# Levels two and four tiles behind as overlaid broadcast rows in a gated linear attention layer on one Trainium2 core

## The chip, the cores and the metric

The kernel runs on one core of one Trainium2 chip, in one launch. Its engines are TensorE (PE, with its weight loads shown as PEld), VectorE (DVE), ScalarE (ACT), GpSimd (POOL) and SyncE (SP), which here only issues DMAs. The metric is the device time of the launch in microseconds, lower is better. The kernel before takes 1411.46 us, the median of 3 runs (1408.34 to 1414.47).

## The reference

Input x is 8 sequences of 1024 tokens with 128 features. Per sequence, with 8 heads of size 128 and 12 decay levels:

```python
q, k, v = x @ Wq.T, x @ Wk.T, x @ Wv.T            # per head 128 wide; x is layernormed first
g   = -softplus(x @ Wg.T + bg);  G = cumsum(g)     # one gate per head
lam = softplus(x @ Wdl.T + Lparam)                 # one weight per head and level
lvl[t, s] = 0 if t == s else floor(log2(t - s)) + 1
A[t, s] = (q[t] . k[s]) / sqrt(128) * exp(G[t] - G[s]) * lam[t, lvl[t, s]]   for s <= t
out = layernorm((A @ v) @ Wo.T + x) * ln_g + ln_b;  x = x0 + out
# then a second layernorm, a gate over 8 experts (top 2, renormalized) and the weighted sum of their linear maps
```

What matters here is the weight W[t, s] = exp(G[t] - G[s]) * lam[t, lvl]. The kernel makes its logarithm and takes one exp. A tile of 128 keys times 128 queries that lies d tiles behind the diagonal holds levels as follows: d = 0 and 1 hold many; d = 2 holds levels 8 and 9 (distances under and from 256), d = 3 holds level 9 alone, d = 4 holds levels 9 and 10 (distances under and from 512). Tiles five and more behind hold level 10 alone and are handled by running states.

## The kernel before

The sequences are a batch loop b of 8, the heads a loop of 8 inside it, 64 heads in all, numbered n. The work of a head is cut into 12 groups (GROUPS: one key tile and up to 512 queries; nine of them are SPLIT and computed in high and low parts, three are FULL and 128 wide), and each group into 4 places, so a head has 48 places and a sequence 384. Each engine runs its own program over the same places; tables written out by hand (U_AT, FAR_AT, V_AT, PE_MORE, DVE_MORE, ACT_MORE, POOL_MORE) say at which place it does an extra piece. Engines are in order, and semaphores join them. Per group: PE makes scores (`scores`, L1523 to L1525 or L1577) into one of two banks s_ps; DVE multiplies them with the weights (`weigh`, L1150) into one of 7 buffers a; ACT rounds them (`high_a`, L892); POOL subtracts (`low_a`, L692); PE multiplies with the values (`values`, L1603 or L1598) LAG = 6 groups behind the scores.

The weights w of head n+1 are made while head n runs. `unit(n, u)` on PE (L1546) builds the logarithms by small fp16 matmuls against masks into l_ps, in four units: d = 0 (16 matmuls), d = 1 (16), d = 2 (8, 96 columns) and d = 4 (8, 64 columns). `exps(n, u)` on ACT (L844) turns each tile into w by one exp of 128x128 with the key's bias: 8, 7, 6 and 4 of them. For d = 3 no matmul is needed: `far_exps` (L855) does 5 exps from a row of logarithms that a DMA spreads over all partitions (far, 320 KB). The operands of the matmuls are small tables (ra, rc, rb) gathered by 8, 8 and 16 DMAs a head from scratch in DRAM (`load_low`, L456; `load_rb`, L469), all issued by SP in the order of `load_levels`, three heads ahead; `load_next_farther` (L483) waits for cq_done, which PE gives at place 41 (`state_values`, L1625). DVE's first `weigh` of a head waits until all exps of that head are done.

Once per sequence the pieces of the tables run: layernorm statistics (`first_statistics`, `second_statistics`, L1163), `take_y` on ACT (L941, waits for the output store of the sequence before last), the gates of the experts (`gates`, L1333 to L1359), softplus, sums, logs, decays, `low_logs` (L1249) on DVE, and 16 pieces `add_up` (`up`, L1376 and L1379).

Of the kernel before, what the change touches and what calls it, by code (L numbers as in the profile page):

```python
# [22 lines left out]
H = 8  # L23
# [27 lines left out]
F16 = mybir.dt.float16  # L51
BF16 = mybir.dt.bfloat16
# [20 lines left out]
UNITS = [[(0, 0, 8)], [(1, 1, 7)], [(2, 2, 6)], [(4, 4, 4)]]  # L73
# [13 lines left out]
def constants():  # L87
# [38 lines left out]
def program(nc, x, Wq, Wk, Wv, Wg, bg, Wdl, Lparam, Wo, ln_g, ln_b, fWg, fbg, fWe, fbe, masks, table, out):  # L126
# [4 lines left out]
    eb_dram = nc.dram_tensor("eb_scratch", [B, H * HIGH, 2, T], F16, kind="Internal").ap()  # L131
    ef_dram = nc.dram_tensor("ef_scratch", [B, HIGH * H + H, NF], F32, kind="Internal").ap()

    with ExitStack() as outer:
# [15 lines left out]
        def m(name, rows_=P):  # L150
# [3 lines left out]
                   m_dram, n_dram, ea_dram, eb_dram, ef_dram, cst, mask, m, c, rows,  # L154
# [6 lines left out]
LAG = 6  # L161
# [19 lines left out]
HALF_B = TB // 2  # L181
# [16 lines left out]

PE_MORE = {4: [('Y', 0)], 33: [('Y', 1)], 59: [('T', 0)], 87: [('Z', 0)], 93: [('T', 1)], 118: [('Z', 1)],
# [14 lines left out]
ACT_MORE = {8: [('y', 0)], 32: [('t_apply', 0)], 36: [('y', 1)], 47: [('t_apply', 1)], 54: [('t_apply', 3)],  # L214
            56: [('t_apply', 2), ('t_high', 0)], 107: [('t_high', 1)], 112: [('apply2', 0)], 122: [('x_high', 0)],
            123: [('apply2', 3), ('x_high', 1)], 132: [('abs', 0)], 145: [('num', 0)], 159: [('exp', 0)],
            171: [('ln', 0)], 198: [('lnl', 0)], 217: [('l_high', 0)], 239: [('l_high', 1)], 328: [('ek', 0)]}
POOL_MORE = {23: [('t_dev', 0)], 41: [('xb', 0), ('dev1', 0)], 43: [('apply1', 1), ('apply1', 0)],
             54: [('apply1', 2)], 55: [('apply1', 3)], 60: [('scale', 0)], 75: [('scale', 1), ('xb', 1)],
             78: [('add', 0)], 82: [('add', 1)], 93: [('dev2', 0)], 103: [('apply2', 1)], 121: [('apply2', 2)],  # L220
             268: [('total', 0)], 301: [('base', 0)], 374: [('total', 1)], 376: [('base', 1)]}
# [50 lines left out]
def main_stage(nc, x, Wq, Wk, Wv, Wg, bg, Wdl, Lparam, Wo, ln_g, ln_b, fWg, fbg, fWe, fbe, masks, table, out,  # L272
# [3 lines left out]
    with ExitStack() as ctx:  # L276
# [1619 lines left out]
```

## Time and profile before

| | before |
|---|---|
| median of 3 runs | 1411.46 us |
| profiled execution, its own time | 1405.15 us |
| span of the profiled execution | 1403.3 us |
| PE busy | 1299.5 us (93%), 10278 matmuls |
| PEld busy | 1137.4 us (81%) |
| DVE busy | 1082.8 us (77%), 2724 instructions |
| ACT busy | 1104.5 us (79%), 3270 instructions |
| POOL busy | 792.7 us (56%), 956 instructions |
| mean granted clock of PE | 0.987 |
| moved by DMA | 80.37 MB, mean 57 GB/s |

The profile is of one execution. Busy time is the union of an engine's instructions; matmuls are pipelined and their ends are modelled, so a PE that is busy all the time may still wait, and starts tell more than lengths. "Idle before" is charged to whatever released the engine. In steady state one sequence of 8 heads repeats every 165.3 us.

### The profile page before, as it was taken

The page shows a single profiled execution, that of the slowest core. Times are in us where ns is not written, and L with a number is a line of the kernel's source. Part 1 is how long each engine was busy: PE and PEld are TensorE (multiplying, and loading weights), DVE is VectorE, ACT ScalarE, POOL GpSimd, SP SyncE. Part 2 cuts the span into 40 slices and gives each one's busy share as a digit, 9 for nine tenths or more (in the row PEclk, how much of TensorE's full clock was granted, in tenths as well). Part 3 has the DMA queues.
Part 4 walks back from the last instruction along what each step waited for, and adds up shares of the span by engine and source line. Part 5 has one row for each costly group of instructions (what it writes and reads, how often), then busy time and mean ns, then how long its engine had stood idle before and what let it go on. Part 6 is the DMA issues. An engine that isn't in the chain of part 4 may idle for free.

```text
span 1403.3 us, 31442 instructions
## 1 busy us (share of the span) xinstructions
PE 1299.5 (93%) x10278; PEld 1137.4 (81%) x10278; DVE 1082.8 (77%) x2724; ACT 1104.5 (79%) x3270; POOL 792.7 (56%) x956
## 2 busy tenths in 40 slices
PE   4699899999999999999999999999999999989997
PEld 4588788888888788787888888887888878878875
DVE  4767767798868977689777988679886797767776
ACT  3589879888788877897788977888778887778732
POOL 2154457734585455953578444864558545595562
PEclk9899999999999999999999999999999999999998
DMA  5311122112221121111221122211212112211200
GB/s 180 113 45 51 43 70 70 42 43 59 58 72 44 50 73 54 44 50 44 73 73 50 44 58 58 67 44 37 71 46 73 50 44 59 72 45 30 67 9 16
DMA packets 125725, 80.37 MB, mean 57 GB/s; under 512 B 50569, under 2 KB 115323, under 8 KB 125435
## 3 DMA queue, kind: packets, MB, share of 16 engines
q1 hardware_dynamic: 124472, 77.85, 20.2%
q8 instruction: 83, 1.36, 0.4%
q10 hardware_dynamic: 1090, 0.51, 0.2%
q14 instruction: 80, 0.65, 0.2%
HBM read 67.64 MB, written 10.09 MB: 55 GB/s over the span
## 4 chain that ended last, share of the span: by engine, by line
PE 47%; ACT 16%; DVE 12%; POOL 11%; SPq 6%; issue 4%; DMA 3%; ACTq 0%; POOLq 0%; DVEq 0%
PE o_ps L1603 11%; ACT w_all L844 6%; PE s_ps L1523 4%; PE l_ps L1546 4%; PE aux L1523 4%; PE s_ps L1525 4%; PE s_ps L1524 4%; POOL a_lo_all L692 4%; PE aux L1524 3%; PE aux L1525 3%; SPq L456 3%; ACT a_hi L892 3%; DVE a_all L1150 2%; PE aux L1616 2%; SPq L469 2%
## 5 line engine op out<-in xcount | busy, mean ns | idle before, releaser
L692 POOL TENSOR_TENSOR a_lo_all<-a_all,a_hi 128x256 fp32r<-128x256 f32 (+2 forms) x576 | 575.5, 1016 | 526.2 <-ACT a_hi L892 524.4
L844 ACT ACTIVATE w_all<-l_ps,bias 128x128 f32<-128x128 f32 x1589 | 439.3, 388 | 43.8 <-PE l_ps L1546 42.4
L1150 DVE TENSOR_TENSOR a_all<-s_ps,w_all 128x512 f32<-128x512 f32 (+3 forms) x768 | 360.6, 483 | 132.6 <-PE s_ps L1525 87.9
L1603 PE MATMUL o_ps<-a_hi,v_all 128*128 128x256 f32 (+2 forms) x1152 | 396.7, 353 | 1.7 <-POOL a_lo_all L692 1.7
L892 ACT ACTIVATE a_hi<-a_all 128x256 fp32r<-128x256 f32 (+2 forms) x576 | 300.1, 547 | 75.5 <-DVE a_all L1150 73.7
L1523 PE MATMUL s_ps<-q_hi,xt_hi 128*128 128x256 f32 (+2 forms) x576 | 224.8, 390 | 31.1 <-DVE a_all L1150 29.3
L1603 PEld LDWEIGHTS o_ps<-a_hi,v_all 128*128 128x128 f32 x1152 | 218.1, 189 | 23.1 <-POOL a_lo_all L692 1.8
L1525 PE MATMUL s_ps<-q_hi,xt_lo 128*128 128x256 f32 (+2 forms) x576 | 195.1, 339 | 0.0
L1524 PE MATMUL s_ps<-q_lo,xt_hi 128*128 128x256 f32 (+2 forms) x576 | 194.7, 338 | 0.0
L1603 PE MATMUL o_ps<-a_lo_all,v_all 128*128 128x256 f32 (+2 forms) x576 | 194.4, 338 | 0.0
L1523 PEld LDWEIGHTS s_ps<-q_hi,xt_hi 128*128 128x128 f32 x576 | 109.8, 191 | 43.9 <-DVE a_all L1150 22.8
L884 ACT ACTIVATE v_all<-aux 128x512 fp32r<-128x512 f32 x124 | 79.1, 638 | 56.7 <-PE aux L1525 56.7
L1603 PEld LDWEIGHTS o_ps<-a_lo_all,v_all 128*128 128x128 f32 x576 | 109.8, 191 | 11.5
L1525 PEld LDWEIGHTS s_ps<-q_hi,xt_lo 128*128 128x128 f32 x576 | 108.9, 189 | 7.9
L1076 DVE CAST q_hi<-aux 128x512 fp32r<-128x512 f32 x128 | 88.0, 687 | 35.2 <-PE aux L1525 34.8
L1379 DVE SCALAR_TENSOR_TENSOR late<-aux,gl,late 128x128 f32<-128x128 f32 x392 | 110.8, 342 | 5.4 <-PE aux L1525 5.4
L1524 PEld LDWEIGHTS s_ps<-q_lo,xt_hi 128*128 128x128 f32 x576 | 110.1, 191 | 4.6
L855 ACT ACTIVATE w_all<-far,bias 128x128 f32<-128x128 f32 x320 | 101.0, 413 | 0.0
L1119 DVE TENSOR_TENSOR v_all<-aux,v_all 128x512 fp32r<-128x512 f32 x128 | 87.5, 684 | 7.1 <-ACT v_all L884 6.8
L1089 DVE TENSOR_TENSOR q_lo<-aux,q_hi 128x512 fp32r<-128x512 f32 x128 | 88.5, 691 | 4.4
L1523 PE MATMUL aux<-nt,xt_hi 128*128 128x256 f32 x256 | 73.1, 286 | 10.6 <-DVE tx L1249 3.8
L1577 PE MATMUL s_ps<-q_full,x_full 128*128 128x128 f32 x384 | 79.6, 289 | 1.5 <-DVE a_all L1150 1.5
(259 smaller groups left out, 2617.5 us busy)
## 6 DMA issues: line engine op xcount, KB each, us to landing
far<-ef_scratch SPq DMA_DIRECT2D x64, 320.0 KB, 3.6
rb<-eb_scratch SPq DMA_DIRECT2D x1016, 0.8 KB
farther<-ef_scratch SPq DMA_DIRECT2D x64, 192.0 KB, 3.3
ra<-ea_scratch SPq DMA_DIRECT2D x508, 4.0 KB, 2.1
rc<-ea_scratch SPq DMA_DIRECT2D x508, 4.0 KB, 1.6
mt<-m_scratch SPq DMA_DIRECT2D x62, 128.0 KB, 3.5
nt<-n_scratch SPq DMA_DIRECT2D x62, 128.0 KB, 3.5
tx<-in_L_attn_x SPq DMA_DIRECT2D x9, 512.0 KB, 5.6
```

What stands on the lines that cost most here:

```text
L692: pool.tensor_tensor(a_lo[r][:, 0:t1 - t0], a[r][:, 0:t1 - t0], a_hi[r][:, 0:t1 - t0].bitcast(F32), ALU.subtract).then_inc(a_lo_done, 1)
L844: last = act.activation(w[k][:, W_AT[j] + d, :].rearrange("p (f c) -> p f c", f=2), l_tiles[:, :, :, i - i0], ACT.Exp, bias=bias[b % 2][:, ...
L855: last = act.activation(w[k][:, W_AT[j] + FAR0, :], far[k][:, j * P:(j + 1) * P], ACT.Exp, bias=bias[b % 2][:, h, BIAS_AT[FAR0] + j:BIAS_A ...
L892: act.activation(a_hi[r][:, 0:t1 - t0], a[r][:, 0:t1 - t0], ACT.Copy).then_inc(a_hi_done, 1)
L1076: dve.tensor_copy(q_hi[n % 2][:, cols], bank(piece)).then_inc(q_hi_done, 1)
L1089: dve.tensor_tensor(q_lo[n % 2][:, cols], bank(piece), q_hi[n % 2][:, cols].bitcast(F32), ALU.subtract).then_inc(freed(piece), 1)
L1150: dve.tensor_tensor(a[(n * NG + g) % NA][:, 0:t1 - t0], s_ps[:, g % 2, 0:t1 - t0], w[n % 2][:, at:at + (t1 - t0) // P, :].rearrange("p i n ...
L1379: ins = dve.scalar_tensor_tensor(acc[:, i, :], bank(piece)[:, k * P:(k + 1) * P], gl[0][:, i, ex:ex + 1], acc[:, i, :], ALU.mult, ALU.add)
L1523: pe.matmul(o, a_hi, hi, start=True, stop=False)
L1524: pe.matmul(o, a_hi, lo, start=False, stop=False)
L1525: return pe.matmul(o, a_lo, hi, start=False, stop=True)
L1603: last = pe.matmul(o, lhs[:, vr, j, :], rhs[r][:, 0:t1 - t0], start=fresh, stop=True, skip_group_check=True)
```

## The change

Five things change together.

1. The units d = 2 and d = 4 on PE, their tables rb, masks mb2 and mb4, scratch eb, their 16 DMAs a head and their exps from PSUM go. In their place three rows of logarithms (levels 8, 9 and 10, of 6, 6 and 4 tiles: row8, row9, row10) are spread over all partitions by three DMAs a head, into one buffer each (before: two buffers of far).
2. DVE overlays: by `copy_predicated` with a fixed 128x128 mask of bytes it writes the level 9 row over row8 (6 tiles, 768 elements a partition) where the distance is in level 9, and over row10 (4 tiles, 512 elements) where it is still in level 9. It does so once each a head, at places 20 and 15.
3. ACT does 5, 6 and 4 exps from row9, row8 and row10 (`row_exps`) after groups 3, 6 and 9; before, 6 and 4 from PSUM and 5 from far. The next rows are fetched only when all three sets of exps of the head before are done.
4. LAG is 7 and there are 8 buffers each of a, a_hi and a_lo.
5. All tables of places are new. `low_logs` and `level_high` have one part instead of two.

```diff
-LAG = 6
+LAG = 7
-UNITS = [[(0, 0, 8)], [(1, 1, 7)], [(2, 2, 6)], [(4, 4, 4)]]
+UNITS = [[(0, 0, 8)], [(1, 1, 7)]]
-U_AT = {0: 0, 3: 1, 5: 2, 8: 3}
-FAR_AT = {8: 0}
-B_AT = {21: 0}
-X_AT = {41: 0}
+U_AT = {0: 0, 4: 1}
+FAR_AT = {3: 0, 6: 1, 9: 2}
+SEL_AT = {15: 1, 20: 0}
+B_AT = {12: 0}
+X_AT = {46: 0}
-        rb = [sb(f"rb{k}", [KB, TB, NTB, NC], F16) for k in range(2)]
-        far = [sb(f"far{k}", [P, NF]) for k in range(2)]
+        row8, row9, row10 = sb("row8", [P, NR]), sb("row9", [P, NR]), sb("row10", [P, NT4])
+        after, until = (sb(n, [P, P], U8) for n in ("after", "until"))
-        def load_far(eng, n):
+        def load_rows(eng, n):
             b, h = divmod(n, H)
+            for level, row in ((8, row8), (9, row9), (10, row10)):
+                at = NR - row.shape[1]
+                eng.dma_start(row[:, :], ef_dram[b, h * HIGH + level - LOW, at:].partition_broadcast(P)).then_inc(rows_in, 16)
-                    load_rb(sp, n, range(TB))
-                    if n >= 2:
-                        sp.wait_ge(far_done, n - 1)
-                    load_far(sp, n)
+                def load_next_rows(n):
+                    sp.wait_ge(far_done, NFAR * n)
+                    sp.wait_ge(t["stored"], EL * (n // H + 1))
+                    load_rows(sp, n)
@@ SP, head n: after load_m(n + 3) and, at head 4, store_el(b + 1)
+                        load_next_rows(n + 2)
                         load_next_farther(n + 2)
@@ ScalarE
+                def row_exps(n, part):
+                    d, row = ((3, row9), (NEAR, row8), (TOP, row10))[part]
+                    if part == 0:
+                        act.wait_ge(rows_in, ROWS_IN * (n + 1))
+                    else:
+                        act.wait_ge(selected[part - 1], n + 1)
+                    first = NC - row.shape[1] // P
+                    for j in range(NC - d):
+                        at = (j + d - first) * P
+                        last = act.activation(w[k][:, W_AT[j] + d, :], row[:, at:at + P], ACT.Exp,
+                                              bias=bias[b % 2][:, h, BIAS_AT[d] + j:BIAS_AT[d] + j + 1])
+                    last.then_inc(far_done, 1)
@@ VectorE
+                def select_rows(n, part):
+                    dst, src, where = ((row8, row9, after), (row10, row9, until))[part]
+                    dve.wait_ge(rows_in, ROWS_IN * (n + 1))
+                    tiles = dst.shape[1] // P
+                    dve.copy_predicated(dst[:, :].rearrange("p (i n) -> p i n", n=P),
+                                        where[:, None, :].broadcast_to([P, tiles, P]),
+                                        src[:, NR - tiles * P:].rearrange("p (i n) -> p i n", n=P)).then_inc(selected[part], 1)
@@ places in a sequence of 384 (head h is 48h to 48h+47), those the prediction speaks of
 DVE  stat1(2) 42 -> 41; gate(3) 181 -> 192; softplus 185, 186 -> 178; up(0) 190 -> 195; guard 195 -> 190; up(3) 240 -> 233
 ACT  take_y(1) 36 -> 40; abs 132 -> 144; exp 159 -> 146
 POOL dev2 93 -> 104; apply2(1) 103 -> 105; scale(1) 75 -> 67; add 78, 82 -> 71, 78
```

## Rows read from the trace of the kernel before

**Rows 1.** Windows: one sequence by head, from first weigh to first weigh, busy us per engine.

```profile
378.50:397.00 18.50, 17.08 (x158) 15.21 (x156) 13.49 (x36) 15.64 (x48) 14.69 (x21) 1.00 0.29 82
397.00:418.70 21.70, 19.92 (x156) 17.91 (x156) 14.25 (x34) 19.79 (x62) 20.98 (x30) 1.00 0.18 52
418.70:438.70 20.00, 19.07 (x163) 16.93 (x162) 13.83 (x32) 15.93 (x49) 15.73 (x25) 1.00 0.19 51
438.70:460.90 22.20, 20.92 (x181) 18.52 (x182) 21.27 (x51) 21.75 (x60) 9.62 (x10) 1.00 0.12 35
460.90:483.10 22.20, 20.55 (x158) 17.47 (x157) 21.28 (x56) 18.12 (x48) 8.96 (x10) 1.00 0.14 36
483.10:504.10 21.00, 20.20 (x148) 17.72 (x149) 17.21 (x45) 17.34 (x54) 7.53 (x9) 1.00 0.22 56
504.10:523.00 18.90, 18.90 (x149) 16.49 (x148) 14.93 (x39) 13.86 (x46) 13.46 (x14) 1.00 0.36 102
523.00:543.80 20.80, 20.80 (x168) 18.41 (x166) 16.98 (x44) 15.21 (x49) 7.93 (x8) 1.00 0.13 42
sum 165.30, PE 157.44 PEld 138.65 DVE 133.24 ACT 137.65 POOL 98.91; mean PE 19.68 PEld 17.33 DVE 16.66 ACT 17.21 POOL 12.36
```

**Rows 2.** Chain of waits, end of head 7 to head 0: start us, us, what.

```profile
541.60 0.32 SPq L483
...
550.54 0.32 SPq L469
...
557.59 3.52 DMA out<-late
```

**Rows 3.** Timeline of ScalarE and VectorE, head 0: start us, us, instruction, [idle before].

```profile
557.68 1.12 ACT L844 ACTIVATE w_all<-l_ps,bias 128x128 f32<-128x128 f32 x4
558.68 1.57 ACT L855 ACTIVATE w_all<-far,bias 128x128 f32<-128x128 f32 x5
...
561.82 0.49 DVE L1163 BATCH_NORM_STATS2 e_st<-late 128x6 f32<-128x128 f32 x2 [3.45 <-ACT late L941]
```

**Rows 4.** Timeline of TensorE around the units d = 2 and d = 4.

```profile
802.44 0.50 PE L1546 MATMUL l_ps<-rb,mask 96*128 96x96 f16 x8 [0.38 <-ACT w_all L844]
802.77 0.42 PE L1523 MATMUL s_ps<-q_hi,xt_hi 128*128 128x384 f32 x1
...
807.01 0.41 PE L1546 MATMUL l_ps<-rb,mask 96*128 96x64 f16 x8
807.26 0.42 PE L1523 MATMUL s_ps<-q_hi,xt_hi 128*128 128x384 f32 x1
```

**Rows 5.** Timeline of VectorE and GpSimd in gate(3), head 3.

```profile
454.90 0.23 DVE L1357 TENSOR_TENSOR gl<-gl 128x64 f32<-128x64 f32 x1
454.97 2.54 POOL L692 TENSOR_TENSOR a_lo_all<-a_all,a_hi 128x512 fp32r<-128x512 f32 x2 [1.72 <-ACT a_hi L892]
...
455.15 1.18 DVE L1358 TENSOR_TENSOR gl<-gl 128x64 f32<-128x64 f32 x1
...
456.37 1.22 DVE L1359 TENSOR_TENSOR gl<-gl,gm 128x64 f32<-128x64 f32 x1
```

**Rows 6.** VectorE by line and shape: busy us, mean ns of one, idle before.

```profile
L1379 DVE SCALAR_TENSOR_TENSOR late<-aux,gl,late 128x128 f32<-128x128 f32 x392 | 110.8, 342 | 5.4 <-PE aux L1525 5.4
...
L1249 DVE TENSOR_TENSOR tx<-aux,tx 24x512 f16<-24x512 f32 x16 | 11.2, 697 | 0.5
...
L1194 DVE TENSOR_SCALAR z<-z 128x704 f32<-128x704 f32 x8 | 7.1, 890 | 0.0
...
L1302 DVE TENSOR_TENSOR late<-late,w_all 128x512 f32<-128x512 f32 x1 | 0.7, 693 | 0.0
```

**Rows 7.** Waits: who waited for whom, us in total, times, longest.

```profile
DVE e_st L1163 <- POOL late L727: 16.9, 14, 3.7
```

**Rows 8.** DMA issues by line: KB each, median us to landing.

```profile
far<-ef_scratch SPq DMA_DIRECT2D x64, 320.0 KB, 3.6
...
m_scratch<-late SPq DMA_DIRECT2D x1, 1024.0 KB, 5.3
```

More of the change, by code:

```diff
@@ L77 @@
 _at = 0
-for _name, _n in (("ma0", NTA * P), ("ma1", NTA * P), ("mb2", NTB * P), ("mb4", NTB * P),
-                  ("ident", P), ("tri", P), ("suf", P), ("first", E), ("off", TA)):
+for _name, _n in (("ma0", NTA * P), ("ma1", NTA * P), ("ident", P), ("tri", P), ("suf", P), ("first", E), ("off", TA)):
     CONST[_name] = (_at, _at + _n)
@@ L153, in program @@
         main_stage(nc, x, Wq, Wk, Wv, Wg, bg, Wdl, Lparam, Wo, ln_g, ln_b, fWg, fbg, fWe, fbe, masks, table, out,
-                   m_dram, n_dram, ea_dram, eb_dram, ef_dram, cst, mask, m, c, rows,
+                   m_dram, n_dram, ea_dram, ef_dram, cst, mask, m, c, rows,
                    wet_hi, wet_lo, fwg2, wcat)
 MEAN_VAR = 6
-LAG = 6
+LAG = 7
 NA = LAG + 1
@@ L214 @@
[L214 to L221, printed above, removed]
+U_AT = {0: 0, 4: 1}
@@ L272, in main_stage @@
 def main_stage(nc, x, Wq, Wk, Wv, Wg, bg, Wdl, Lparam, Wo, ln_g, ln_b, fWg, fbg, fWe, fbe, masks, table, out,
-               m_dram, n_dram, ea_dram, eb_dram, ef_dram, cst, mask, m, c, rows,
+               m_dram, n_dram, ea_dram, ef_dram, cst, mask, m, c, rows,
                wet_hi, wet_lo, fwg2, wcat):
@@ L291, in main_stage @@
         rc = [sb(f"rc{k}", [P, TA, NTA, NC], F16) for k in range(2)]
[L292 to L295 removed]
+        row8, row9, row10 = sb("row8", [P, NR]), sb("row9", [P, NR]), sb("row10", [P, NT4])
+        after, until = (sb(n, [P, P], U8) for n in ("after", "until"))
+        farther = [sb(f"farther{k}", [P, NQ]) for k in range(2)]
         q_hi = [sb(f"q_hi{k}", [P, T], F32R) for k in range(2)]
@@ L848, in exps @@
                     last.then_inc(w_done, 1)
-                def far_exps(n):
+                def row_exps(n, part):
                     k = n % 2
                     b, h = divmod(n, H)
-                    act.wait_ge(far_in[k], 16 * (n // 2 + 1))
-                    for j in range(NC - FAR0):
-                        last = act.activation(w[k][:, W_AT[j] + FAR0, :], far[k][:, j * P:(j + 1) * P], ACT.Exp,
-                                              bias=bias[b % 2][:, h, BIAS_AT[FAR0] + j:BIAS_AT[FAR0] + j + 1])
+                    d, row = ((3, row9), (NEAR, row8), (TOP, row10))[part]
[8 more added lines that the diff above has]
+                                              bias=bias[b % 2][:, h, BIAS_AT[d] + j:BIAS_AT[d] + j + 1])
                     last.then_inc(far_done, 1)
@@ L1037, in _ @@
                 farther_exps(0)
-                far_exps(0)
+                for part in range(NFAR):
+                    row_exps(0, part)
                 act.wait_ge(s_rows, 1)
@@ L1476, in _ @@
                     first_v(u)
+                dve.wait_ge(preds, 2)
+                for part in range(2):
+                    select_rows(0, part)
                 for u in range(Q_U):
@@ L1491, in _ @@
                             first_query(1, late[:, 1, 0:NQ])
+                        if place in SEL_AT and n + 1 < NH:
+                            select_rows(n + 1, SEL_AT[place])
                         if place in C_OUT:
@@ L1837, in _ @@
                         turn_expert_weights()
-                    if u < 2:
-                        value(0, u + 2)
-                    if u in (2, 3):
-                        scores(0, u - 2)
-                    if u == 3:
-                        for k in range(Q_U):
-                            query(1, k)
+                    value(0, u + 2)
+                for g in range(2):
+                    scores(0, g)
+                for k in range(Q_U):
+                    query(1, k)
                 wait_taken(pe, ("q", 1, 0))
```

148 lines of the change are left out of this document (61 added, 87 removed), and 14 rows, old and new, of tables (DVE_MORE, PE_MORE).

## The prediction

> **What bounds the kernel now.** I read the windows first, cut at the first weigh of each head, since shares over the whole span mix stages. The steady sequence of 8 heads takes 165.30 us, and no engine fills it: PE is busy 157.44, ACT 137.65, DVE 133.24, POOL 98.91 [rows 1]. By head the reader is to see four kinds of stage. Heads 5, 6 and 7 are PE's: 20.20 of 21.00, 18.90 of 18.90, 20.80 of 20.80. Heads 3 and 4 are DVE's: 21.27 and 21.28 of 22.20, though in head 3 ACT is just as full (21.75) and PE is not far below (20.92). Head 1 is POOL's, 20.98 of 21.70. Head 0 belongs to nobody: 18.50 us, PE 17.08.
>
> The chain of waits shows what is odd about head 0. From the last state matmul of head 7 it runs down SP's queue: farther at 541.60, sixteen issues for ra and rc, sixteen for rb from 550.54, then far and nt, then the output store issued at 557.59, which lands 3.52 us later; `take_y` on ACT waits for that [rows 2]. On the other side DVE stands idle for 3.45 us at 561.82, behind nine exps on ACT that end near 560.25 and then take_y [rows 3]. One head on, the second statistics on DVE wait for POOL, 16.9 us in 14 times, so 2.4 us in each of seven sequences [rows 7]. PE's clock is at full speed in all eight windows (1.00) [rows 1], so it is no term.
>
> **The change part by part.** I count in us per sequence and multiply at the end.
>
> *PE, units d = 2 and d = 4.* The d = 2 unit starts at 802.44 and the next matmul at 802.77, so 0.33; d = 4 goes from 807.01 to 807.26, 0.25 [rows 4]. That is 0.58 a head of pure PE time. It counts fully where PE is the bound, heads 5, 6, 7: 3 x 0.58 = 1.74. The unit d = 2 also waited 0.38 for ACT to empty l_ps [rows 4]; with two units, 16 places apart, I take this as gone in those heads for another 0.3. Sum -2.0. In exchange these heads get two selects each; DVE is at 14.93 of 18.90 in head 6 and 16.98 of 20.80 in head 7 [rows 1], and 1.6 more fits, though head 7 then has only about 1.6 us of air.
>
> *DVE, the selects.* The trace has no copy_predicated. It reads a mask and a source, both in SBUF, and writes 768 and 512 elements a partition. The nearest rows are a two-input subtraction-like operation from SBUF of 512 elements, 693 ns, and a one-input one of 704 elements, 890 ns: 1.03 ns per element between them, so 0.69 and 0.96 by length [rows 6]. Back to back, operations here start about 0.08 before the previous one's end, so 0.6 + 0.87 = 1.47 a head. Bounds: from below, a copy at two elements per cycle would halve it to 0.75; from above, if it had to go over the destination as well at two cycles an element, 2.9. I take 1.47, the rows' own rate.
>
> On top comes what the rows of gate(3) show. A tiny 64-element operation took 0.23 us at 454.90 before POOL began its subtraction at 454.97; the next two, just as small, took 1.18 and 1.22, and each ended when one of the two POOL subtractions did (2.54 for both) [rows 5]. All have both inputs in SBUF, as the selects do. POOL is busy 98.91 of 165.30, 60% [rows 1], but groups 3 and 4, at places 12 to 19 where the selects lie, are FULL and give it nothing to subtract. So I add 0.15, with bounds 0 and 2 x 1.27 a head. The price of a select pair is 1.6 us.
>
> The Trainium skill, "SBUF — State Buffer", section "SBUF: two separate sides", has the rule behind this and it speaks against the change: VectorE with two SBUF inputs and GpSimd take one shared pair of ports by an exclusive lock, held for the whole instruction, so the later one fully blocks. The trace agrees (0.23 against 1.18 and 1.22). By the rule the pair would also block POOL in return for 1.47 us a head.
>
> *DVE, heads 3 and 4.* Here DVE time is kernel time. Head 4 gets a select pair (1.6). By the new places it also gets gate(3), up(0) and up(3), and gives guard to head 3 (its row is the 890 ns one [rows 6]). gate(3) now costs about 3 us (its last three operations run from 454.90 to 457.59, and two small ones stand before them) [rows 5], of which nearly 2 is blocking by POOL; at place 192 POOL has less to do, so I take 2.0. An up is four operations of 342 ns that overlap by 0.08, 1.05 each [rows 6]. `low_logs` loses its 24-row part, 0.70 [rows 6]. Head 4: +1.6 + 2.0 + 1.05 + 1.05 - 0.8 - 0.7 = +4.2, of which 0.9 finds the idle time that head 4 has (22.20 - 21.28): +3.3, rounded up to 3.6 since such a full engine never packs perfectly (it is 96% full now). Head 3 loses 3.0 + 1.05 and gains 0.8 + 1.6, so DVE falls to about 19.7, but ACT with 21.75 [rows 1] and PE stay where they were. I give it 0. The ten exps that move from PSUM to SBUF cost ACT more: four from PSUM take 1.12, five from far 1.57, that is 0.25 against 0.29 apart [rows 3], 0.4 a head, hidden except perhaps in head 3.
>
> *Head 0.* SP's queue loses 16 issues: 550.54 to about 556.0, 5.4 us [rows 2]. It waits for cq_done five places later (some 2 us), and three row issues go earlier, under that wait. The store would be issued near 553.7 and land near 557.3 instead of 561.1. Then ACT is the last: its exps before take_y are now 4 instead of 9, but take_y comes four places later. What is late next is ACT's own exps, about 1 us behind DVE. Of the 3.45 idle I take 2.0 as saved: -2.0.
>
> *Head 1.* POOL's dev2, some 4 us, goes to head 2, and the two adds go 4 to 7 places forward, so the 2.4 of waiting shrinks; LAG 7 lets POOL be one group later before PE notices. PE's 19.92 [rows 1] less 0.6 is the floor. I take -1.2. *Head 2* takes dev2: POOL 15.73 + 4, near the 20.00 of the head, so it gains nothing: 0.
>
> *LAG 7 elsewhere, start, end.* PE almost never waited for POOL's subtraction, so the extra buffer is worth nothing where the trace has no such wait; the eighth group at the very end and the two selects at the start lie in waits for DMAs. 0, bounds -3 and +3 in all.
>
> *Sum.* -2.0 (heads 5 to 7) + 3.6 (head 4) + 0 (head 3) - 2.0 (head 0) - 1.2 (head 1) + 0 = -1.6 a sequence. The stretch from first weigh to tail is 1295.7 us, 7.84 sequences of 165.30: -12.5. The profiled execution's own time is 1405.15, so 1392.6. The median shown, 1411.46, is 1.0045 times that: 1399.
>
> **The rivals.**
>
> *Head 4 doesn't fill up.* If gate(3) isn't blocked at its new place (its five operations at about 0.2 are 1.0, not 2.0), head 3 gives back what DVE loses there down to PE's 20.3 (-1.9), and head 4 costs 2.2: -2.0 + 2.2 - 1.5 - 2.0 - 1.2 = -4.5 a sequence, -35, so about 1376. For it: DVE ran without gap through head 3. Against: ACT's 21.75 in the same window [rows 1].
>
> *The selects block (slower).* One mechanism: the longer operation finds POOL in a subtraction almost each time, 1.27 us for each [rows 5], and holds POOL afterwards. A pair is then 1.47 + 2 x 1.0 = 3.5 instead of 1.6. Heads 3 and 4 pay 1.9 each less 2.5 of air in head 3, head 7 pays 3.5 less the 3.2 it has left after the unit, head 1's gain goes: about +3.5 on my sum, +1.9 a sequence, +15, so 1426. It decides from a pair above 2.4 us. An operation at two cycles an element has the same price (2.9), and the two together 1440. For it: rows 5; the rule of the skill named above gives this time if DVE and POOL meet at random. Against: the places chosen lie in POOL's pause.
>
> *Rows land late (slower).* There is one buffer, so the fetch waits for the exps at place 38, and DVE needs it at place 15 of the next head, 25 places or some 10.8 us later, less ACT's lag of 2 to 3. The three DMAs carry 1024 KB; one such DMA lands in 5.3, three of far's 3.6 in a row would be 10.8 [rows 8]. At 5.3 it is hidden; behind a store of tables (head 4, once a sequence) it is late by 1 to 2 us. If it were late at every head by 0.5, +4 a sequence: 1430. DMA share is only 0.12 to 0.36 [rows 1], which speaks against it.
>
> *No net effect.* Head 4 costs all the other heads give: 5.2 instead of 3.6, so about 0: 1411.
>
> **How the numbers follow.** A measurement of this kernel can tell about 0.5% from no change, 7 us, so faster means under 1404. Chances: my forecast 0.36 (its own range 1390 to 1408; 0.30 faster, 0.06 same), head 4 not full 0.18 (faster), no net effect 0.16 (0.12 same, 0.02 each side), selects block 0.18 and rows late 0.12 (both slower). Faster 0.50, same 0.18, slower 0.32. The range reaches from below the first rival, where the low bound of the select (0.75) would add a few us, to the two slower ones with part of the high bound: 1368 to 1434.
>
> **What would show it.** L1546 falls to 32 matmuls a head, and the chain at the sequence's start no longer holds 16 issues of rb. The selects show 0.95 and 0.69 us in DVE's groups if the rate is right, with maxima near 2 if POOL blocks them. Head 4's window grows to about 26 us with DVE above 95%, head 3 stays near 22, heads 5 to 7 sum to about 58.7, and the DVE idle before e_st behind ACT falls from 3.45 to under 1.5. A wait of DVE or ACT on the rows' DMA in most heads would make me wrong by the third rival; a pair over 2.4 us by the second; a head 4 under 24 us by the first.

## The result: 1.7% slower

The changed kernel takes 1435.5 us, the median of 4 runs (1434.29 to 1437.03), beside 1410.98 for the kernel before on the same chip: a ratio of 1.0173, 95% interval 1.0148 to 1.0198. The forecast was 1399.0 with a range up to 1434, so sign and range are both missed. The profiled execution has a span of 1433.2 us, against 1403.3.

The windows of the same sequence, cut at the first weigh of each head, answer to [rows 1]. Columns: stretch, its length, then busy us of PE, PEld, DVE, ACT and POOL, then TensorE's granted clock, DMA share and GB/s.

```profile
380.70:398.20 17.50, 16.25 (x124) 13.93 (x122) 15.82 (x42) 14.12 (x43) 16.30 (x21) 1.00 0.45 134
398.20:420.50 22.30, 20.21 (x143) 18.37 (x139) 15.74 (x36) 20.52 (x63) 21.07 (x30) 0.92 0.20 66
420.50:440.00 19.50, 18.50 (x148) 16.59 (x146) 16.05 (x34) 16.19 (x49) 17.44 (x26) 1.00 0.33 87
440.00:464.80 24.80, 22.35 (x175) 19.07 (x174) 22.48 (x50) 22.11 (x59) 10.83 (x11) 1.00 0.25 76
464.80:489.90 25.10, 19.98 (x117) 17.04 (x118) 24.30 (x62) 18.33 (x47) 9.39 (x9) 0.90 0.16 54
489.90:512.70 22.80, 22.47 (x157) 19.25 (x156) 17.23 (x44) 17.27 (x55) 9.00 (x9) 0.96 0.41 117
512.70:530.80 18.10, 17.84 (x131) 15.57 (x129) 16.51 (x42) 13.07 (x40) 11.48 (x12) 1.00 0.36 95
530.80:552.20 21.40, 21.09 (x169) 18.69 (x169) 18.23 (x45) 17.09 (x52) 8.27 (x9) 1.00 0.24 78
sum 171.50, PE 158.68 PEld 138.50 DVE 146.35 ACT 138.68 POOL 103.77; mean PE 19.83 PEld 17.31 DVE 18.29 ACT 17.34 POOL 12.97
```

Head by head against [rows 1] that is -1.0, +0.6, -0.5, +2.6, +2.9, +1.8, -0.8, +0.6: +6.2 in this sequence. The second to the seventh sequence together are 32.7 us longer than before (5.4 each), the first is 3.0 shorter. PE is busy 1.2 us longer although its units are gone, and its clock is below 1.00 in three heads, where it was 1.00 in all. DVE has 13.1 more.

The selects and two small operations, of the level logs (L1231) and of the gates (L1348), VectorE by line and shape (busy us, mean ns, idle before):

```profile
L1145 DVE COPY_PREDICATED row<-after,row 128x768 f32<-128x768 uint8 x64 | 69.2, 1081 | 0.0
...
L1145 DVE COPY_PREDICATED row<-until,row 128x512 f32<-128x512 uint8 x64 | 64.6, 1010 | 5.3 <-DMA row<-ef_scratch 5.2
...
L1231 DVE TENSOR_TENSOR z<-lz,run 128x96 f32<-128x96 f32 x16 | 16.2, 1014 | 0.0
...
L1348 DVE TENSOR_TENSOR gm<-gm 128x8 f32<-128x8 f32 x8 | 8.1, 1018 | 0.0
```

The durations of a pair add up to 2.09 us on the mean. The next fence is the timeline of VectorE and GpSimd at the pair of head 0 (start us, us, instruction).

```profile
384.44 3.44 POOL L675 TENSOR_TENSOR a_lo_all<-a_all,a_hi 128x512 fp32r<-128x512 f32 x3
...
385.70 1.62 DVE L1145 COPY_PREDICATED row<-until,row 128x512 f32<-128x512 uint8 x1
...
387.22 0.27 DVE L1137 TENSOR_TENSOR a_all<-s_ps,w_all 128x128 f32<-128x128 f32 x1
...
387.81 1.00 DVE L1145 COPY_PREDICATED row<-after,row 128x768 f32<-128x768 uint8 x1
```

The shorter select takes 1.62 us while POOL subtracts, the longer one 1.00 behind it. The small operations of L1231 and L1348 took 302 and 157 ns before the change. They take 1013 and 1019 ns in tiny_select too, the run without the selects below, so their growth comes with the new places and not with the selects.

Of the waits (who for whom, us in total, times, longest), these answer to [rows 3, 7] and to a wait of ScalarE on VectorE's weighing that was 73.7 us in 105 times:

```profile
ACT a_hi L880 <- DVE a_all L1137: 156.6, 124, 2.9
...
ACT farther L849 <- DMA farther<-ef_scratch: 22.5, 23, 2.6
...
DVE e_st L1158 <- ACT late L928: 10.1, 8, 1.4
...
DVE e_st L1158 <- POOL late L710: 5.6, 4, 2.7
```

The chain of waits, by engine, shows who took over; PE had 47% of it and DVE 12:

```profile
DVE 34%; PE 27%; ACT 15%; POOL 13%; issue 5%; DMA 4%; SPq 1%; ACTq 0%; DVEq 0%; POOLq 0%
```

The lower clock is seen in TensorE's timeline in head 4. The engine first stood for 2.15 us, waiting for VectorE's `up`; then matmuls of 512 columns start 0.43 apart, and 0.23 apart once the clock is back. The two windows behind the timeline give the granted clock: 0.99 up to 467.70, and 0.51 (1.2 GHz for nearly all of it) in the 3.4 us after:

```profile
466.62 0.66 PE L1674 MATMUL aux<-z,cst 128*128 128x64 f32 x4 [2.15 <-DVE late L1372]
...
467.83 0.63 PE L1523 MATMUL aux<-xt_hi,mt 128*128 128x512 f32 x1
468.26 0.63 PE L1524 MATMUL aux<-xt_lo,mt 128*128 128x512 f32 x1
...
476.51 0.39 PE L1523 MATMUL s_ps<-q_hi,xt_hi 128*128 128x512 f32 x1
476.74 0.39 PE L1524 MATMUL s_ps<-q_lo,xt_hi 128*128 128x512 f32 x1
```

```profile
464.40:467.70 3.30, 1.15 (x10) 1.08 (x10) 3.23 (x10) 2.13 (x8) 1.35 (x2) 0.99 0.85 299
467.70:471.10 3.40, 3.40 (x11) 2.83 (x11) 3.23 (x11) 3.36 (x7) 1.00 (x1) 0.51 0.05 9
```

### The profile page after: what moved, and what is told of

Its sections match the earlier page's. It is cut to its first block, busy times and chain, and to the rows that moved or that the text cites. A ratio compares the mean times of both kernels' runs of the same rounds, so it can differ in the third digit from the quotient of the medians.

```text
span 1433.2 us, 28570 instructions
## 1 busy us (share of the span) xinstructions
PE 1293.8 (90%) x9254; PEld 1125.0 (78%) x9254; DVE 1190.7 (83%) x2838; ACT 1110.8 (78%) x3254; POOL 826.8 (58%) x954
## 4 chain that ended last, share of the span: by engine, by line
DVE 34%; PE 27%; ACT 15%; POOL 13%; issue 5%; DMA 4%; SPq 1%; ACTq 0%; DVEq 0%; POOLq 0%
DVE a_all L1137 6%; PE o_ps L1593 5%; POOL a_lo_all L675 5%; DVE late L1372 4%; ACT w_all L843 4%; DVE row L1145 4%; ACT a_hi L880 3%; PE aux L1523 3%; PE s_ps L1523 2%; DVE q_hi L1063 2%; PE s_ps L1525 2%; PE s_ps L1524 2%; PE aux L1524 2%; PE aux L1525 2%; DVE q_lo L1076 2%
## 5 line engine op out<-in xcount | busy, mean ns | idle before, releaser
L675 POOL TENSOR_TENSOR a_lo_all<-a_all,a_hi 128x256 fp32r<-128x256 f32 (+2 forms) x576 | 585.2, 1036 | 545.4 <-ACT a_hi L880 545.2
L880 ACT ACTIVATE a_hi<-a_all 128x256 fp32r<-128x256 f32 (+2 forms) x576 | 293.2, 534 | 157.5 <-DVE a_all L1137 156.6
L843 ACT ACTIVATE w_all<-row,bias 128x128 f32<-128x128 f32 x960 | 301.9, 404 | 3.4 <-DVE row L1145 3.2
L826 ACT ACTIVATE w_all<-l_ps,bias 128x128 f32<-128x128 f32 x953 | 258.9, 384 | 12.9 <-PE l_ps L1542 12.4
L1523 PE MATMUL s_ps<-q_hi,xt_hi 128*128 128x256 f32 (+2 forms) x576 | 225.2, 391 | 24.2 <-DVE a_all L1137 22.1
L1593 PEld LDWEIGHTS o_ps<-a_hi,v_all 128*128 128x128 f32 x1152 | 222.5, 193 | 21.7 <-POOL a_lo_all L675 1.6
L1524 PE MATMUL s_ps<-q_lo,xt_hi 128*128 128x256 f32 (+2 forms) x576 | 198.1, 344 | 0.0
L1525 PE MATMUL s_ps<-q_hi,xt_lo 128*128 128x256 f32 (+2 forms) x576 | 198.0, 344 | 0.0
L1523 PEld LDWEIGHTS s_ps<-q_hi,xt_hi 128*128 128x128 f32 x576 | 110.7, 192 | 46.2 <-DVE a_all L1137 32.7
L1523 PE MATMUL aux<-nt,xt_hi 128*128 128x256 f32 x256 | 80.5, 315 | 23.3 <-DVE q_lo L1076 14.7
L1567 PEld LDWEIGHTS s_ps<-q_full,x_full 128*128 128x128 f32 x384 | 67.7, 193 | 16.6 <-DVE a_all L1137 4.3
```

Source lines behind the costliest of these rows:

```text
L675: pool.tensor_tensor(a_lo[r][:, 0:t1 - t0], a[r][:, 0:t1 - t0], a_hi[r][:, 0:t1 - t0].bitcast(F32), ALU.subtract).then_inc(a_lo_done, 1)
L826: last = act.activation(w[k][:, W_AT[j] + d, :].rearrange("p (f c) -> p f c", f=2), l_tiles[:, :, :, i - i0], ACT.Exp, bias=bias[b % 2][:, ...
L843: last = act.activation(w[k][:, W_AT[j] + d, :], row[:, at:at + P], ACT.Exp, bias=bias[b % 2][:, h, BIAS_AT[d] + j:BIAS_AT[d] + j + 1])
L880: act.activation(a_hi[r][:, 0:t1 - t0], a[r][:, 0:t1 - t0], ACT.Copy).then_inc(a_hi_done, 1)
L1523: pe.matmul(o, a_hi, hi, start=True, stop=False)
L1524: pe.matmul(o, a_hi, lo, start=False, stop=False)
```

## The experiments

Each kernel is the changed one with one edit, unless it says otherwise; ratios are to the kernel before, measured beside it at 1410 to 1413 us. Windows are those of the third sequence, heads 0 to 7. The diffs are shortened: `...` and the comments stand for what is left out.

**tiny_select: what are the selects worth?**

```diff
-dve.copy_predicated(dst..., where..., src...).then_inc(selected[part], 1)
+dve.tensor_copy(dst[:, 0:1], src[:, 0:1]).then_inc(selected[part], 1)
```

> The kernel after with each of the two selects a head replaced by a copy of one element a partition (the overlay is left out); waits, DMAs, exps and places stay. Theory A, the selects' time on VectorE sets the end (134 us of it in the profile after, 1081 and 1010 ns each): the time falls from 1435 by more than half of that, to 1350 to 1370, below before. Theory B, the new places, the late farther row and the lower clock set it: the selects matter little, 1415 to 1430.

1396.41 us, 0.9902 (0.9879 to 0.9925). So the pair costs 39 us, of the 134 us that it is busy, and all else in the change gains 1%. (The run leaves the overlay out; its result serves to time the rest.) The gain is not where I had put it: windows 16.1, 20.4, 18.9, 24.9, 25.1, 22.1, 17.5, 20.8, a sum of 165.8 against 165.3 before. The second to the seventh sequence take 2.5 us more in all than before; the first is 5.5 shorter, the end from the last sequence's first weigh 3.4. Heads 3 and 4 are as long without the selects as with them.

**reduce_select: length or blocking?** Reductions to a maximum, over the same 768 and 512 elements, with one input.

```diff
-dve.copy_predicated(dst..., where..., src...)
+dve.tensor_reduce(red_out[...], src[:, NR - tiles * P:]..., AX, ALU.max)
```

> The selects replaced by maximum reductions that read the same 768 and 512 elements a partition from one SBUF operand and write almost nothing (the overlay is left out). Same length without a second SBUF input. Theory A1, blocking between VectorE and GpSimd is the price: operations fall to about 0.95 and 0.70 us, GpSimd's subtractions of 256 fall back from 770 to 742 ns, and the time is 15 to 30 us below after, 1405 to 1420. Theory A2, plain length is the price: within 7 us of after, 1428 to 1436.

1409.27 us, 0.9989 (0.9972 to 1.0007). The reductions take 942 and 677 ns, about as long as unblocked selects (least 992 and 720). Something of this length costs 13 us (1396 to 1409). The other 26 go with what a select has and a reduction lacks: the second SBUF input that can meet POOL, the row that it writes, and 0.17 us more a pair even when nothing blocks it (1.04 and 0.75 against 0.94 and 0.68). The run doesn't tell these apart, so it is not shown that blocking alone costs 26.

**old_places and farther_21.** The old tables with LAG 6, and the exp of farther (the row of weights with which a query reads the running states) alone back at place 21.

```diff
-LAG = 7                 # old_places, with all tables that both kernels have
+LAG = 6
-B_AT = {12: 0}          # farther_21, this alone
+B_AT = {21: 0}
```

> The kernel after with LAG 6 and the tables of places of the kernel before (all but U_AT, FAR_AT and the places of the selects). Theory B, the new places overfill heads 3 to 5: 1400 to 1415, with head 4 back near 23 us. Theory A, the selects: no better than after, 1430 to 1445, because the selects cost the same wherever the rest stands.

> The kernel after with one change: ScalarE's exp of the farther row at place 21 of a head instead of 12. In the profile after ScalarE waits 22.5 us in 23 times for that DMA at place 12, and the chain goes through it. If this wait is on the path: 8 to 15 us less, 1420 to 1427. If ScalarE has the time to spare: within 4 us of after.

1468.22 us, 1.0409 (1.0385 to 1.0433), and 1507.13, 1.0675 (1.063 to 1.0721). The new places help. farther_21 made a new wait that I had not foreseen, since VectorE takes the query two places behind:

```profile
DVE farther L1072 <- ACT farther L849: 59.0, 33, 4.2
```

Heads 1 and 2 grew from 22.3 and 19.5 to 26.3 and 24.7; heads 3 and 4 stayed at 25.0 and 24.9.

**dve_back, tiny_dve_back, old_pieces, lag_6: what lengthens heads 3 and 4?**

```diff
# DVE_MORE, dve_back (and tiny_dve_back, with tiny_select's edit)
+181: [('gate', 3)], 190: [('up', 0)], 195: [('guard', 0)], 240: [('up', 3), ('l_low', 1)]
-190: [('guard', 0)], 192: [('gate', 3)], 195: [('up', 0)], 233: [('up', 3)]
# old_pieces: PE_MORE, DVE_MORE, ACT_MORE, POOL_MORE of before; lag_6: LAG = 6
```

> The changed kernel with four pieces back at the old kernel's places on VectorE: gate(3) at 181, up(0) at 190, guard(0) at 195, up(3) at 240; nothing else is altered. In the kernel with the selects left out, heads 3 and 4 still took 24.9 and 25.1 us (22.2 and 22.2 before the change), so the selects do not lengthen them. Theory A (head 4 is long because VectorE got gate(3) and up(3) there): head 4 loses their 1.4 + 1.3 us, of which the idle 0.8 us is already left, so 2 us, 7 times, 14 us: 1421 us. Rival (heads 3 to 5 are long through the places of the pieces within every head, and what VectorE does not do in head 4 it does in head 3): the same within 5 us, 1430 to 1438.

> dve_back with the two selects replaced by copies of one element (the overlay of levels 8 and 10 with 9 is left out). The two cures together, if they add: 1396 - 14 = 1382 by theory A, 1396 by the rival. If VectorE's load in head 4 is the bound there only together with the selects, dve_back gains and this one does not.

> The changed kernel with the old kernel's four tables of a sequence's once-only pieces (PE_MORE, DVE_MORE, ACT_MORE, POOL_MORE), and the new tables within a head and LAG 7 kept. Theory A (the new places of these pieces put 6.8 us on heads 3 to 5 and take 6.2 off heads 0 to 2 and 6, through queues that the pieces lengthen): heads 3 and 4 return to about 22.5 us and heads 0, 1, 6 grow by 1 us each: the time falls by some 2 us a sequence, 1420. Rival (the tables within a head do it: row exps behind the selects, farther's exp at place 12): heads 3 and 4 stay near 25, and heads 0 to 2 lose their gain: 1450.

> The changed kernel with LAG 6, that is seven tiles of weighted scores and values six groups behind. Theory A (the deeper queue hides VectorE's late weighing, which the selects cause): every head in which a select comes at a stall grows by up to a group, 8 heads by 0.5 us: 1435 + 30 = 1465. Rival (the queue's depth is nothing once the engines are full): 1435.

dve_back 1452.85 us, 1.0303 (1.0271 to 1.0335); tiny_dve_back 1383.46, 0.9798 (0.9774 to 0.9822); old_pieces 1447.13, 1.025 (1.0226 to 1.0274); lag_6 1433.23, 1.0155 (1.0134 to 1.0176).

The same edit gives 13 us without the selects and costs 17 with them: the pair is worth 69 us there. What differs is who meets whom. gate(3)'s last two operations, first in dve_back, then in tiny_dve_back:

```profile
L1351 DVE TENSOR_TENSOR gl<-gl 128x64 f32<-128x64 f32 x8 | 8.8, 1095 | 0.3
...
L1352 DVE TENSOR_TENSOR gl<-gl,gm 128x64 f32<-128x64 f32 x8 | 8.5, 1068 | 0.3
```

```profile
L1350 DVE TENSOR_TENSOR gl<-gl,gm 128x64 f32<-128x64 f32 x8 | 2.8, 346 | 0.3
...
L1349 DVE TENSOR_TENSOR gl<-gl 128x64 f32<-128x64 f32 x8 | 2.8, 344 | 0.3
```

With the pair, they fall into a row of three POOL subtractions, and TensorE stands behind them. Timeline of dve_back, head 3:

```profile
466.90 3.44 POOL L675 TENSOR_TENSOR a_lo_all<-a_all,a_hi 128x512 fp32r<-128x512 f32 x3 [3.17 <-ACT a_hi L880]
...
467.03 1.22 DVE L1351 TENSOR_TENSOR gl<-gl 128x64 f32<-128x64 f32 x1
...
468.28 1.19 DVE L1352 TENSOR_TENSOR gl<-gl,gm 128x64 f32<-128x64 f32 x1
...
469.50 0.69 DVE L1106 TENSOR_TENSOR v_all<-aux,v_all 128x512 fp32r<-128x512 f32 x1
...
470.25 0.39 PE L1523 MATMUL aux<-nt,xt_hi 128*128 128x256 f32 x1 [3.06 <-DVE v_all L1106]
```

That head takes 26.9 us at a clock of 0.89, against 23.4 at 0.93 in tiny_dve_back. old_pieces brings head 4 to 21.3 with the pair in it (25.1 in the changed kernel), so head 4's length is the pieces' doing; but heads 0, 2, 5 and 6 grow by 1.1, 0.9, 1.5 and 1.8. LAG is worth nothing.

**before_pair: the pair in the kernel before.** Two selects of 640 elements on level 9's row, in place, so that the values stay.

```diff
+dve.copy_predicated(row, pick[:, None, :].broadcast_to([P, NF // P, P]), row).then_inc(selected[part], 1)
+SEL_AT = {15: 0, 20: 1}
```

> The old kernel with two selects of 640 elements added in every head (at places 15 and 20, in place in the buffer of level 9's far row, so that the values stay what they are), 1280 elements in all as in the change. Its units of distance 2 and 4 stay on TensorE. Theory A (a VectorE at 83% has no place left where such a pair is free, whatever the other engines do; without its pair the changed kernel was 39 us faster): 1410 + 40 = 1450. Rival (the pair is dear only in the new schedule, whose TensorE and ScalarE wait for VectorE's weighing; in the old one the heads 0 to 2 and 5 to 7 have VectorE idle for 4 to 7 us each): only heads 3 and 4 grow, by 1.7 us each, 8 times: 1410 + 27 = 1437 at most, and near 1420 if head 3 has room.

1464.17 us, 1.0381 (1.0358 to 1.0404): +53 us, with TensorE's units still there. By head, from [rows 1]: +1.1, +1.2, +0.1, +2.5, +0.5, +0.8, +0.9, +0.8. The chain of waits in head 6 (start us, us, what), where the kernel before has VectorE busy for 14.93 of 18.90:

```profile
531.12 0.42 DVE a_all L1154
...
534.43 1.02 DVE far L1164
...
536.65 0.80 DVE far L1164
...
539.92 0.56 DVE a_all L1154
540.48 0.04 issue
540.52 0.50 PE s_ps L1541
```

For 9.4 us the chain does not leave VectorE, and both selects are on it. The kernel before is already full at that point of its head 6; its own windows show it, 7.49 busy of 8.00, then 5.50 of 7.70 (third number after the length, behind PE and PEld):

```profile
507.30:515.30 8.00, 8.00 (x65) 6.88 (x64) 7.49 (x20) 5.24 (x18) 5.61 (x7) 1.00 0.05 10
515.30:523.00 7.70, 7.70 (x56) 6.84 (x55) 5.50 (x17) 5.42 (x17) 4.65 (x5) 1.00 0.47 136
```

**only_512, only_768, select_apart, split.**

```diff
# only_512: the 768 is a copy of one element; only_768: the 512 is
-SEL_AT = {15: 1, 20: 0}
+SEL_AT = {18: 0, 30: 1}                     # select_apart
+SEL_AT = {15: (0, 0), 19: (0, 2 * P), 23: (0, 4 * P), 27: (1, 0), 31: (1, 2 * P)}   # split
```

> The changed kernel with the select of 768 elements replaced by a copy of one element (level 8's row is not overlaid), the one of 512 kept. By length 768 is 60% of the pair's 39 us: 1435 - 24 = 1411. By blocking (the 768 ran at 1.04 us nearly everywhere, the 512 was blocked in heads 0, 2, 6 and 7) the 768 is worth less: 1435 - 15 = 1420.

> The changed kernel with the select of 512 elements replaced by a copy of one element (level 10's row is not overlaid), the one of 768 kept. By length: 1435 - 16 = 1419. By blocking: 1435 - 24 = 1411.

> The changed kernel with the two selects apart, the 768 first: SEL_AT = {18: 0, 30: 1} instead of {15: 1, 20: 0}; each still comes before its row's exps at places 26 and 38. Theory A (two selects close together make VectorE late by 2 us at once, more than the queue of two score banks hides): 1435 - 10 = 1425. Rival (what counts is VectorE's total, and the row exps now wait for the later select): 1435 to 1445.

> The changed kernel with each select cut into pieces of 256 elements, level 8's three at places 15, 19 and 23, level 10's two at 27 and 31. Five instructions instead of two cost VectorE some 0.2 us more by their fixed part. Theory A (the places are full up to group 8, whatever the burst): 1430 to 1445. Rival (it is the burst of 1 us in front of a weighing, against two score banks, that stalls TensorE): heads 0 to 2 and 5 to 7 get half of their 5.7 us a sequence back: 1413.

only_512 1405.45 us, 0.9958 (0.9941 to 0.9975); only_768 1407.62, 0.9985 (0.9971 to 0.9998); select_apart 1434.84, 1.0171 (1.0146 to 1.0195); split 1453.9, 1.0297 (1.0275 to 1.0319). Each select alone costs 9 to 11 us, both 39: the price is not that of the work. Nor is it that of blocking by itself, for alone the 512 and the 768 take 1.07 and 1.21 us on the mean, longer than in the pair (1.01 and 1.08). I read it as the price of what no longer fits, where the second finds nothing left; no run shows the wait at which the two meet. Taking them apart changes nothing. Cut up they cost 18 us more, as pieces of 256 elements still take 0.62 and 0.64 us each.

**before_pair_late, select_late: another place?** In before_pair the selects at 36 and 40 and the far exps at 42; in the changed kernel at 34 and 40.

```diff
+SEL_AT = {36: 0, 40: 1}; FAR_AT = {10: 0}                    # before_pair_late
+SEL_AT = {34: 0, 40: 1}; FAR_AT = {4: 0, 9: 1, 10: 2}        # select_late
```

> before_pair (1464 us, 53 over the old kernel, 8.0 us a sequence: heads 0 to 2 +2.4, heads 3 and 4 +3.1, heads 5 to 7 +2.6) with the two selects at places 36 and 40 and the far row's exps at place 42 instead of 34. Theory A (VectorE is full in the groups 3 to 8 of a head and half idle in the groups 9 to 11: in heads 0 to 2 these last 5.2 us with 2.5 us of work, in heads 5 to 7 4.1 us with 3.1): heads 0 to 2 pay nothing, 5 to 7 half, 3 and 4 all: 4.4 us a sequence, 53 x 4.4 / 8.0 = 29: 1440 us. Rival (the total of VectorE's work or GpSimd's blocking sets the price): 1464 as before, or more, since the exps then stand late.

> The changed kernel with the selects at places 34 and 40 and the row exps at places 18, 38 and 42 (SEL_AT = {34: 0, 40: 1}, FAR_AT = {4: 0, 9: 1, 10: 2}). Theory A: heads 0 to 2 and 5 to 7, whose selects cost 5.7 us a sequence, keep half of that: 1435 - 22 = 1413. Rival (the rows' buffers are single: fetched only behind the last exps, now 4 places later, and the four exps of level 10 then stand at the head's end before the first weighing): 1435 to 1450.

1488.44 us, 1.0543 (1.0516 to 1.057), and 1561.14, 1.1052 (1.1031 to 1.1072): the theory of the free end of the head failed as a cure. In heads 0, 1, 5, 6 and 7 the late pair is indeed cheaper than the early one (18.8, 22.4, 20.8, 19.5, 21.3 against 19.6, 22.9, 21.8, 19.8, 21.6), but heads 2, 3 and 4 go from 20.1, 24.7, 22.7 to 21.5, 27.0, 23.6. In select_late TensorE waits for single weighings up to 8.7 us:

```profile
PE s_ps L1567 <- DVE a_all L1137: 76.2, 47, 8.7
```

One cause is the late exps, which may hold back the next head's weighing; this was not tried by itself. Another stands in the trace: at its late place the longer select itself takes nearly twice as long as at place 20 (1.08 us):

```profile
L1145 DVE COPY_PREDICATED row<-after,row 128x768 f32<-128x768 uint8 x64 | 122.3, 1911 | 0.0
```

In before_pair_late, too, a select takes 1.20 us on the mean, against 1.02 in before_pair. So the late places were not free of POOL, and neither run is a clean test of idle time at the head's end.

**half_old, half_new, half_new_back: half of the change, all of the computation.** From the kernel before: distance 4 by row and select, distance 2 on TensorE.

```diff
-UNITS = [[(0, 0, 8)], [(1, 1, 7)], [(2, 2, 6)], [(4, 4, 4)]]
+UNITS = [[(0, 0, 8)], [(1, 1, 7)], [(2, 2, 6)]]
+FAR_AT = {8: 0, 9: 1}; SEL_AT = {29: 0}     # half_old; half_new has the new tables
+sp.wait_ge(ten_done, n)                     # ahead of the row's fetch, in SP's queue
```

> Half of the change on the old kernel, the whole computation done: distance 4 by a broadcast row of level 10 overlaid with level 9 by one select of 512 elements at place 29 and four exps at place 38; distance 2 stays on TensorE; the old places and LAG 6. Theory A (VectorE's places are full, and one select costs the old kernel its share of 53 us: 53 x 512 / 1280 = 21, less if the first is cheap as in the new one, 9 to 11; the unit of distance 4 gives back 0.25 us of TensorE in each head, 16 us where TensorE ends last): 1410 + 21 - 16 = 1415, and 1405 if the first select is cheap. Rival (the gone unit gives nothing back, as TensorE waits for VectorE's weighing): 1431.

> The same half of the change with the changed kernel's places (LAG 6; U_AT 0, 4, 7; the far row's exps at place 14, the select at 20, level 10's exps at place 38). only_512, which has one select and no unit of distance 2 at all, took 1405; the unit of distance 2 adds 0.33 us of TensorE in each head and 24 rows of logs to VectorE (0.70 us, twice a sequence): 1405 + 64 x 0.33 x 0.5 + 11 = 1427 if all of the logs' work is on the path, 1416 if none. Rival (the new places fit one select and the unit): under 1405.

> half_new with gate(3), up(0), guard(0) and up(3) back at the old places on VectorE. This gave 13 us without selects and took 17 with two. Theory A (one select is nearer to none): half_new - 5. Rival: half_new + 5 or more.

1465.47 us, 1.0397 (1.0363 to 1.0431); 1467.87, 1.0413 (1.0384 to 1.0442); 1491.87, 1.0576 (1.0549 to 1.0604). Heads 3 to 7 of half_old sum to 105.6 us, against 105.1 before, so there the trade is nearly even. Heads 0 to 2 sum to 65.7 against 60.2. The single row buffer makes SP wait for the last exps (L882, on ScalarE), 214.4 us in 47 times, with all of the next head's loads behind it. SP's waits, and its queue in head 0 of half_old:

```profile
SPq L488 <- ACT w_all L882: 214.4, 47, 12.2
```

```profile
392.98 0.32 SPq L488 DMA_DIRECT2D row<-ef_scratch  x1
...
402.14 5.39 SPq L474 DMA_DIRECT2D rb<-eb_scratch  x16
...
409.25 0.60 SPq L618 DMA_DIRECT2D out<-late  x1
```

The output store goes out 16.1 us into the head. It was 13.8 before [rows 2], and in the changed kernel, without the rb issues, it is 10.0:

```profile
562.15 0.60 SPq L588 DMA_DIRECT2D out<-late  x1
```

None of the eighteen computes everything and beats the kernel before. In eight of them (old_places, farther_21, dve_back, before_pair, split, select_late, half_old, half_new) the time came out 9 to 111 us above everything that I had expected. So the readings above were made after the fact, and no kernel built on them was faster.

## Why the prediction was wrong

**The step that failed** is the sentence on heads 5 to 7, "DVE is at 14.93 of 18.90 in head 6 ... and 1.6 more fits", and its silent twins for heads 0 to 2. I priced the pair at 1.6 us in head 4 and at nothing in the other heads. Against tiny_select the pair costs 1.4, 1.9, 0.6 in heads 0 to 2, nothing in heads 3 and 4, and 0.7, 0.6, 0.6 in heads 5 to 7. The cover was read from averages over heads. In head 6, where it was looked at, VectorE's idle time lay at another point of the head than the places 15 and 20. before_pair shows the price on the kernel before, at 53 us; only_512 and only_768 show that it doesn't add up select by select.

**The price of the pair**, 1.6 us of VectorE's time, was nearly right. The durations add up to 2.09 us, against the 0.96 + 0.69 + 0.15 = 1.80 behind the forecast, but they overlap with their neighbours: over the whole launch VectorE is busy 98.9 us more than in tiny_select, 1.55 a pair, with two copies of 0.14 us in place of each pair, so 1.7 to 1.8. The rate of 1.03 ns an element was right to 10%, as the medians are 1.04 and 0.75 us. What I gave for blocking, 0.15, is about 0.3: all selects together take 133.8 us, and 64 pairs at the medians would take 115, at the least durations (0.99 and 0.72) 110. "The places chosen lie in POOL's pause" was false: places are positions in each engine's order, not times, and POOL still worked on earlier groups (384.44 to 387.88 in the fence above). The rival "the selects block" came near to the time, 1426, but not by its road: it wanted a pair above 2.4 us and heads 3 and 4 paying, and the pair is at 2.09 and these heads paid nothing. The Trainium skill's page "SBUF — State Buffer", section "SBUF: two separate sides", says that VectorE with two SBUF inputs and GpSimd exclude each other for a whole instruction. This trace agrees, with 1.62 against 0.75 us for the same select and 1.22 against 0.23 for a gate operation [rows 5].

**Head 3**, put at 0, is +2.6. **Head 4**, put at +3.6, is +2.9, which is near by luck: 1.6 of the forecast was the pair, which costs nothing there, and 2.0 was gate(3), which never came to head 4: VectorE does the piece of place 192 before the weighing of that place, which ends the window of head 3. `guard` (L1189) and gate(3) (L1348 to L1352) now stand right there, beside a row of four subtractions, and the chain of waits runs through all of them. Timeline of head 3's end in the changed kernel; the last line is head 4's first weighing:

```profile
459.98 4.49 POOL L675 TENSOR_TENSOR a_lo_all<-a_all,a_hi 128x512 fp32r<-128x512 f32 x4 [3.17 <-ACT a_hi L880]
...
461.57 1.26 DVE L1348 TENSOR_TENSOR gm<-gm 128x8 f32<-128x8 f32 x1
...
464.59 0.23 DVE L1352 TENSOR_TENSOR gl<-gl,gm 128x64 f32<-128x64 f32 x1
464.85 0.69 DVE L1137 TENSOR_TENSOR a_all<-s_ps,w_all 128x512 f32<-128x512 f32 x1
```

So VectorE is busy 22.48 us in head 3 where 19.7 was forecast. With the four pieces back and no pair (tiny_dve_back) head 3 takes 22.3 at full clock in the second sequence and 23.4 at 0.93 in the third, as in the kernel before (22.2, and 23.3 at 0.93); in tiny_select it is 24.9 at 0.93. In head 4 the term that I didn't have is the level logs: in tiny_select as in the changed kernel, three small operations grow there from 0.76 to 3.6 us together, and in old_pieces, where they take 0.8, the head is at 21.3. One more `up` adds 1.3, where the forecast had two. What is left of head 3 in the changed kernel, and how the pieces share head 4's 2.9, stays open.

**The clock**, "no term", fell to 0.92, 0.90 and 0.96 in three heads, after stalls such as the 2.15 us above; that one waits for up(0), which VectorE does behind gate(3). In the second to the seventh sequence TensorE runs for some 51 us at 1.2 GHz, against 7 before and 34 in tiny_select. An estimate from the kernel before: in its fifth sequence head 3 has one such stretch of 3.4 us and takes 23.3 us, against 22.2 [rows 1]. The 44 us more at 1.2 GHz would be 13 such stretches, so about 14 us of the 32.7; the 17 us more than in tiny_select would be 5, so about 5 us of the pair's 39. The window of that head:

```profile
769.40:792.70 23.30, 22.20 (x183) 19.86 (x183) 20.55 (x51) 21.84 (x61) 9.43 (x10) 0.93 0.12 33
```

The estimate charges the clock with the stall that brought it down, too. I ran nothing that holds the clock up, so its share is not shown.

**Heads 5 to 7**, put at -2.0 from the units: without the pair +1.1, -1.4, 0.0, so -0.3. What lengthens head 5 stays open. Half of ScalarE's 22.5 us of waiting for farther falls into it (11.5 us in 7 times), but in farther_21, where that wait is gone, the head is no shorter. **Head 1**, put at -1.2, is -1.3 without the pair, and +0.6 with it. **Head 2**, put at 0, is -0.5.

**Head 0** was right in its cause: 16 issues fewer, the store earlier, and the waits before e_st down from 23.4 to 10.1 us for ACT and from 16.9 to 5.6 for POOL. Of the 2.0 us the pair takes half back: -1.0, and -2.4 without it. **LAG 7** at nothing was right (lag_6). **Rows land late** was a small thing: VectorE waits 5.2 us for them in the whole run, and ScalarE the 22.5 us for farther, whose fetch stands behind theirs.

Added up: the pair costs 5.7 us a sequence for 1.6 in the sum, 4.1 too little. The rest of the change was put at -3.2 and is +0.5 in tiny_select, 3.7 off, of which head 3 is 2.7, heads 5 to 7 are 1.7 and head 4 0.9, less 1.6 that heads 0 to 2 did better. Together that is the 7.8 between -1.6 and +6.2. The multiplier of 7.84 was wrong as well: +6.2 in every sequence would have been +49 us, but the profiled execution is 29.9 longer, since the mean of six sequences is +5.4 and the first is shorter.

## What to carry to other kernels

Idle time of an engine is cover only at the place where the new work stands: cut the window at that place, not at the stage. And before adding a two-input operation from SBUF beside a busy GpSimd, try one added to the unchanged kernel; here that single run would have said +53 us, and so the sign, though twice the size. Work added to a nearly full engine has no price of its own: one select cost 10 us, two cost 39 or 69. And a piece belongs to the window in which the engine does it, which the number of its place doesn't tell.

## What was not expected of the hardware

A select of 768 fp32 elements under a byte mask takes 1.04 us and one of 512 takes 0.75, hardly more than a one-input reduction of the same row (0.94 and 0.68). Blocked, the shorter took up to 2.17 us. Very small operations pay as much as long ones: 128x8 took 0.16 us free and 1.26 beside a subtraction. Whether one is blocked depends on when the other engine's work comes: with the four pieces at the same places, the same gate operations took 0.34 us on the mean without the selects and 1.07 to 1.10 with them, and moving the pieces there gained 13 us or lost 17.
